# Second layer of a two-layer transformer kernel: maximum scores in row halves of the array, in a burst of two pairs

## The reference

```
q, k, v = LN(x) @ w_Q, LN(x) @ w_K, LN(x) @ w_V          # 16 heads, head size 8
probs   = softmax(q k^T / sqrt(8))                        # over all 512 keys, no mask
x       = x + probs v
xq      = fp4_quant_dequant(LN(x))                        # blocks of 16
h       = silu(xq @ w_gate^T) * (xq @ w_up^T)             # 352 features
x       = x + fp4_quant_dequant(h) @ w_down^T
```

## Time and profile before

| | us |
|---|---|
| three runs | 2309.03, 2312.15, 2314.53 (median 2312.15) |
| profiled execution | 2317.76 (span 2316.0, first to last instruction) |
| PE busy | 2038.6 (88%) |
| DVE busy | 1621.9 (70%) |
| ACT busy | 1390.4 (60%) |
| POOL busy | 1063.4 (46%) |

### The profile page before, as it was taken

How to read it: one execution, slowest core, us unless ns; L and a number is a source line. 1 busy time by engine, 2 the same in 40 slices (tenths; PEclk the granted TensorE clock), 3 DMA queues, 4 the chain that set the end, 5 groups by cost and what they waited for, 6 DMA issues and landing times.

```text
span 2316.0 us, 45088 instructions
## 1 busy us (share of the span) xinstructions
PE 2038.6 (88%) x13603; PEld 1060.0 (46%) x13603; DVE 1621.9 (70%) x4772; ACT 1390.4 (60%) x3097; POOL 1063.4 (46%) x1777
## 2 busy tenths in 40 slices
PE   2999999999999939999649999999999999999984
PEld 1455455554554429999613333333333333333333
DVE  3888888887888633321137888888888888888854
ACT  0466666666666624444207777777777776777772
POOL 6433746537455250000265656555565655654222
PEclk8899999999999969999859999999999999999997
DMA  5232223223222024444322222121222212121100
GB/s 175 81 93 67 85 74 91 73 71 92 71 89 82 20 73 143 144 142 140 90 73 66 73 58 68 54 62 54 66 59 57 70 55 60 55 64 50 47 6 14
DMA packets 154335, 174.12 MB, mean 75 GB/s; under 512 B 38448, under 2 KB 122096, under 8 KB 153968
## 3 DMA queue, kind: packets, MB, share of 16 engines
q1 hardware_dynamic: 144464, 153.85, 22.6%
q0 software_dynamic: 8192, 16.79, 2.5%
q10 hardware_dynamic: 1440, 0.60, 0.1%
HBM read 120.30 MB, written 49.28 MB: 73 GB/s over the span
## 4 chain that ended last, share of the span: by engine, by line
PE 27%; DVE 12%; issue 5%; ACT 4%; POOL 2%; DMA 0%; SPq 0%; ACTq 0%; DVEq 0%; POOLq 0%
PE bank L1560 8%; PE bank L1538 6%; DVE l_rowmax L1770 6%; PE bank L1548 6%; ACT l_probs L1679 3%; DVE l_h L1790 1%; PE bank L1593 1%; PE bank L1574 1%; DVE l_hq L199 1%; PE bank L1631 1%; DVE l_hq L216 1%; DVE l_stats L1804 1%; DVE l_hq L222 1%; PE bank L1621 1%; PE bank L1579 1%
## 5 line engine op out<-in xcount | busy, mean ns | idle before, releaser
L1770 DVE TENSOR_REDUCE l_rowmax<-bank 128x1 f32<-128x512 f32 x1024 | 642.7, 682 | 109.6 <-PE bank L1538 109.4
L1679 ACT ACTIVATE l_probs<-bank 128x512 f32<-128x512 f32 x1024 | 549.1, 605 | 134.8 <-PE bank L1548 134.5
L865 DVE CUSTOM_DVE_ANT_0 bank<-bank,mask_rows_q 128x512 f32<-128x512 f32 (+3 forms) x1024 | 476.6, 518 | 101.9 <-PE bank L625 95.6
L781 ACT ACTIVATE l_probs<-bank 128x512 f32<-128x512 f32 (+3 forms) x1024 | 389.2, 443 | 150.0 <-PE bank L637 144.0
L1538 PE MATMUL bank<-k_stack,q_stack 96*128 96x512 bf16 x1024 | 395.0, 387 | 68.9 <-DVE l_rowmax L1770 43.9
L1548 PE MATMUL bank<-q_stack,k_stack 128*128 128x512 bf16 x1024 | 387.3, 382 | 1.6 <-ACT l_probs L1679 1.4
L625 PE MATMUL bank<-k_stack,q_stack 96*128 96x512 bf16 (+3 forms) x1024 | 316.8, 314 | 25.4 <-DVE l_rowmax L865 14.8
L635 PE MATMUL bank<-q_stack,k_stack 128*128 128x512 bf16 (+3 forms) x1024 | 307.6, 308 | 0.2
L1560 PE MATMUL bank<-l_probs,v_aug 128*32 128x512 f32 x2048 | 272.8, 605 | 29.4 <-ACT l_probs L1679 28.7
L637 PE MATMUL bank<-mask_rows_k,ident_bf 128*128 128x128 bf16 x1024 | 221.1, 221 | 0.0
L1174 ACT ACTIVATE experts_hT<-bank,experts_b 128x256 f32<-128x256 f32 x288 | 118.3, 471 | 158.2 <-PE bank L1136 158.2
(11 more groups left out here) (259 smaller groups left out, 3015.7 us busy)
## 6 DMA issues: line engine op xcount, KB each, us to landing
q_stack<-scratch SPq DMA_DIRECT2D x384, 96.0 KB
k_stack<-scratch SPq DMA_DIRECT2D x384, 96.0 KB
experts_w<-in_w SPq DMA_DIRECT2D x72, 256.0 KB, 2.4
scratch<-l_q_parts SPq DMA_DIRECT2D x32, 384.0 KB, 2.7
scratch<-l_k_parts SPq DMA_DIRECT2D x32, 384.0 KB, 3.0
experts_rows<-rows_in SPq DMA_DIRECT2D x72, 128.0 KB, 2.1
rows_out<-experts_y SPq DMA_DIRECT2D x72, 128.0 KB, 2.1
q_stack<-l_rowmaxT SPq DMA_DIRECT2D x384, 4.0 KB
```

The costliest lines, as they stand in the source:

```text
L781: nc.scalar.activation(probs[:, (a * HG + j) % PSLOTS, c0:S], bank[:, c0:S], ACT.Exp, scale=SCALE).then_inc(t_read, 1)
L865: nc.vector.tensor_tensor_reduce(scores, scores, m["mask_rows_q"][:, S - keys(t):S], 1.0, LOWEST, ALU.add, ALU.max, rowmax[:, g % 2, c:c + ...
L1679: nc.scalar.activation(probs[:, (a * HG + j) % PSLOTS, :], bank[:, :], ACT.Exp, scale=SCALE).then_inc(t_read, 1)
L1770: nc.vector.tensor_reduce(rowmax[:, g % 2, c:c + 1], bank[:, :], X_AXIS, ALU.max).then_inc(s_read, 1)
```

## The change

1. A head's stack is laid out by its place in the group. Heads 0 and 1 stay as they were. Heads 2 and 3 have their first eight blocks on rows 64 to 127, the ninth on rows 0 to 7, and their maximum on rows 32 to 34. The stack of a group takes 14 DMAs (`stack_parts`) of two heads each instead of six of four heads, and the maximum rows take six (`stack_max`) instead of three. The bytes are the same; the rows copied are 2 KB long instead of 4 KB.
2. The maximum scores use 64 rows: heads j and j + 2 are multiplied one behind the other, the first in rows 0 to 63 and the second in rows 64 to 127 of the array, each into its own bank of a pair of banks. The ninth block (the product of the two smallest parts) is left out of the maximum, not out of the exponential. One DVE instruction reads both banks and writes two maxima.
3. Ring "s" is two pairs of banks, ring "t" has three banks.
4. The order on PE in a slot is: exponential products 0 and 1, both pairs, the MIDDLE table, exponential products 2 and 3, `probs_v` of the slot before, the END table. "out" moves from MIDDLE to END, two up products share a pair of banks and one DVE read, AHEAD is 10, and `rowmax`, `split_max` and `max_out` stand one slot later.
5. In experts, DVE sets the constant rows of heads 2 and 3 with six memsets in four consecutive tiles.

Layer zero keeps its code and its banks.

```diff
+def stack_parts(sp, stacks, scratch, g, stacked):
+    for which, stack in enumerate(stacks):
+        for half in range(2):
+            slots = g * HG + 2 * half
+            base = which * PARTS * P * S + slots * S
+            def copy(row, part, step, blocks):
+                sp.dma_start(stack[row:row + blocks * D, slots:slots + 2, :].rearrange("p h t -> p (h t)"),
+                             bass.AP(scratch.tensor, base + part * P * S, [[step * P * S, blocks], [H * S, D], [1, 2 * S]])
+                             ).then_inc(stacked, 16)
+            for i in range(PARTS):
+                blocks = PARTS if half == 0 or i < PARTS - 1 else PARTS - 1
+                if which == 0:
+                    copy(HALF * half + SLAB * i, i, 0, blocks)
+                else:
+                    copy(HALF * half + SLAB * i, 0, 1, blocks)
+            if half:
+                copy(0, PARTS - 1, 0, 1)
+def stack_max(sp, stack, rowmaxT, g, max_rows):
+    for half in range(2):
+        slots = g * HG + 2 * half
+        for i in range(PARTS):
+            row, src = MAX_ROWS[half] + i, (2 * i + half) * 2 * TT
+            sp.dma_start(stack[row:row + 1, slots:slots + 2, :].rearrange("p h (t q) -> p (h t) q", q=P),
+                         rowmaxT[src:src + 2 * TT, :]).then_inc(max_rows, 16)
...
+S_PAIRS = 2
+T_BANKS_1 = 3
-AHEAD = 9
+AHEAD = 10
...
+            def upper_constants(i):
+                stack = (*m["k_stack"], *m["q_stack"])[i]
+                rows_of = lambda first, end: stack[first:end, :, :].rearrange("p (g j) t -> p g (j t)", j=HG)[:, :, 2 * S:4 * S]
+                nc.vector.memset(rows_of(0, HALF).bitcast(U32), 0).then_inc(stack_set, 1)
+                if i < 2:
+                    dve.wait_ge(stack_set, i + 1)
+                    nc.vector.memset(rows_of(MAX_ROWS[1], MAX_ROWS[1] + PARTS).bitcast(F32), MINUS_ONES)
...
-    MIDDLE = [("rowmax", g, 4 * g + 5) for g in range(G)] + [("out", g, F + 4 * g + 8) for g in range(G)] + [
+    MIDDLE = [("rowmax", g, 4 * g + 6) for g in range(G)] + [
         ("xnT", 0, -15), ("xqT", 0, F + 32)] + [("turn", k, F + 44) for k in range(NC)]
-    END = [("v", 0, 0), ("qk", 0, -9), ("qk", 1, -8)]
-    for t in range(TT):
-        END += [("gate", t, F + 33)] + ([("up", t - 1, F + 33)] if t else [])
-    END += [("up", TT - 1, F + 33), ("down", 0, F + 45), ("down", 1, F + 53)]
+    END = [("out", g, F + 4 * g + 6) for g in range(G)] + [("v", 0, 0), ("qk", 0, -9), ("qk", 1, -8)] + [("gate", t, F + 33) for t in range(2)] + [("up", 0, F + 33)] + [
+        ("gate", t, F + 33) for t in range(2, TT)] + [("up", 1, F + 33), ("down", 0, F + 45), ("down", 1, F + 53)]
...
-    POOL_WORK = [("split_max", g, 4 * g + 4) for g in range(G)]
+    POOL_WORK = [("split_max", g, 4 * g + 5) for g in range(G)]
...
-    SP_WORK = [("max_out", g, 4 * g + 6) for g in range(G)] + [("parts", 0, -6), ("parts", 1, -5)]
+    SP_WORK = [("max_out", g, 4 * g + 7) for g in range(G)] + [("parts", 0, -6), ("parts", 1, -5)]
...
+            def scores_for_max(a, pair):
...
+                banks = s_pair(("max", a, pair))
                 t = TT - 1 - t
-                nc.tensor.matmul(bank[:, :], q_stack[b % 2][0:MAXROW, h_, t * P:(t + 1) * P],
-                                 k_stack[b % 2][0:MAXROW, h_, :], start=True, stop=True).then_inc(s_mm, 1)
+                for half in range(2):
+                    rows, h_ = slice(HALF * half, HALF * (half + 1)), g * HG + pair + 2 * half
+                    last = nc.tensor.matmul(banks[:, half * S:(half + 1) * S], q_stack[b % 2][rows, h_, t * P:(t + 1) * P],
+                                            k_stack[b % 2][rows, h_, :], start=True, stop=True)
+                last.then_inc(s_mm, 1)
...
                     if j == HG // 2:
-                        if uses.exp_quad(s - 1) is not None:
-                            probs_v(uses.exp_quad(s - 1))
+                        if a is not None:
+                            for pair in range(2):
+                                scores_for_max(a, pair)
                         for kind, b, k in due(MIDDLE, s):
...
                     if e is not None:
                         scores_for_exp(e, j)
-                    if a is not None:
-                        scores_for_max(a, j)
+                if uses.exp_quad(s - 1) is not None:
+                    probs_v(uses.exp_quad(s - 1))
                 for kind, b, k in due(END, s):
+                    if kind == "out":
+                        turned_out(b, k)
...
+            def take_max(a, pair):
...
+                largest = rowmax[:, g % 2, :].rearrange("p (k i t) -> p i k t", k=2, t=TT)[:, pair, :, TT - 1 - t]
+                nc.vector.tensor_reduce(largest, banks[:, :].rearrange("p (k n) -> p k n", k=2), X_AXIS, ALU.max).then_inc(s_read, 1)
```

More of the change, by code:

```diff
@@ L255, with __init__ @@
 T_BANKS = 4
-AHEAD = 9
+S_PAIRS = 2
+T_BANKS_1 = 3
+AHEAD = 10
 class Uses:
-    def __init__(self, NB, middle, end, ring_of, first, last, ahead, only):
+    def __init__(self, NB, middle, end, ring_of, first, last, ahead, only, pairs):
         self.NB, self.ahead, self.only = NB, ahead, only
@@ L273, in __init__ @@
                 if j == HG // 2:
+                    if self.max_quad(s) is not None and pairs:
+                        for pair in range(2):
+                            use("s", ("max", self.max_quad(s), pair))
                     for key in self.due(middle, s):
@@ L277, in __init__ @@
                     use("t", ("exp", self.exp_quad(s), j))
-                if self.max_quad(s) is not None:
+                if self.max_quad(s) is not None and not pairs:
                     use("s", ("max", self.max_quad(s), j))
@@ L1590, in turned_out @@
                 pe.wait_ge(oT_ready, b * G + g + 1)
-                bank = s_bank(("out", b, g))
+                bank = s_pair(("out", b, g))
                 for t in range(TT):
@@ L1608, in gate, with up @@
                                  start=True, stop=True).then_inc(t_mm, 1)
-            def up(b, t):
-                bank = s_bank(("up", b, t))
-                nc.tensor.matmul(bank[:, 0:HID], xqT[:, t * P:(t + 1) * P], m["w_in_T"][:, 1, :],
-                                 start=True, stop=True).then_inc(s_mm, 1)
+            def up(b, k):
+                pair = s_pair(("up", b, k))
+                for i in range(2):
+                    t = 2 * k + i
+                    last = nc.tensor.matmul(pair[:, i * S:i * S + HID], xqT[:, t * P:(t + 1) * P], m["w_in_T"][:, 1, :],
+                                            start=True, stop=True)
+                last.then_inc(s_mm, 1)
             def turned_hq(b, k):
@@ L1645, in _ @@
                                 turned_max(b, k)
-                            if kind == "out":
-                                turned_out(b, k)
                             if kind == "xqT":
@@ L1793, in read @@
                         dve.wait_ge(h_scaled, b)
-                    last = hw.largest(tile, k, TT)
-                    if k == TT - 1:
+                    last = hw.largest(tiles, k, 2)
+                    if k == 1:
                         last.then_inc(h_step, 1)
@@ L1811, in _ @@
             for s in slots:
-                for j in range(HG):
-                    if j == HG // 2:
-                        for kind, b, k in due(MIDDLE, s):
-                            if RING[kind] == "s":
-                                read(kind, b, k)
-                    if uses.max_quad(s) is not None:
-                        take_max(uses.max_quad(s), j)
+                if uses.max_quad(s) is not None:
+                    for pair in range(2):
+                        take_max(uses.max_quad(s), pair)
                 for kind, b, k in due(END, s):
@@ L1884, in build @@
         m["experts_loaded"] = mem.sem("experts_loaded")
-        psum = [ctx.enter_context(nc.psum_tensor(f"bank{i}", [P, S], F32)) for i in range(8)]
+        m["bank_pairs"] = [ctx.enter_context(nc.psum_tensor(f"pair{i}", [P, 2 * S], F32)) for i in range(2)]
+        psum = [pair[:, k * S:(k + 1) * S] for pair in m["bank_pairs"] for k in range(2)]
+        psum += [ctx.enter_context(nc.psum_tensor(f"bank{i}", [P, S], F32)) for i in range(4, 8)]
         with ExitStack() as until_experts:
```

88 lines of the change are left out of this document (41 added, 47 removed).

## The result

The changed kernel takes 2295.53 us (median of 5 runs, 2289.19 to 2300.3) against 2314.53 for the kernel before (5 runs on the same chip, 2309.03 to 2316.15): ratio 0.9924, 95% interval [0.9901, 0.9948]. It is faster, by 19 us, where 51 were forecast. The profiled executions are 2295.53 and 2317.76, so the traces have 22.2 us to explain.

A forecast was written before the change was run, and what follows sets the result against it. Gates, then DVE, then PE were taken to bound each period. Terms: periods -54, SP queue +2, start and end +1 and -1, constants +1, sum -51: 2267 us profiled, 2261 median; 8-in-10 range 2230 to 2318.

The forecast's parts named there:

- the limits of the three stretches: In one period: first the gate, SiLU, up chain for 6.5 us, then DVE for 21.5, then PE for 38.6.
- the +2 for the queue of SP at the layer's start: Layer's start: more DMA issue time, partly beside the first stack's landing, makes PE wait +2 us (0 to +5).
- the period of 62.9 us: One 16-slot period: gates 6.6, DVE stretch 22.9, PE stretch 33.4, sum 62.9 us, 3.6 less than 66.57.
- A pair saves 0.25 us a slot: PE slot: overlapping halves, two pairs at 0.22 plus mode changes 0.09 and 0.10, give 2.59 us instead of 2.83.
- The 0.28 for a pair: PE: an estimate from a guide's 3.07 times for four row tiles, adding 0.12 a slot, some 15 us in all.
- A read of two banks starts every 1.14 us: DVE maximum reads: 1.14 us from start to start, so 2.28 a slot against 2.4; bounds 1.07 and 1.20.
- Some 15 such periods: Second layer: some 15 periods, each 3.6 us shorter, giving -54 us.
- The rival *queue of SP: Two groups' stacks, then six maximum rows, issued in sequence make PE wait 5.6 us a period: +84, 2345 us; chance 0.14.
- Constants, +1 (0 to +4): Experts: six memsets of 1.8 us over four tiles; two in one tile outlast a gap, +1 us (0 to +4).
- the halves do overlap: Rival claimed the opposite: halves don't overlap, each PE-stretch slot 0.44 us longer, 62 us in all, 2323; chance 0.08.
- the rows have the mode cost: Rival claimed no mode cost for row tiles: pairs save 0.44 a slot, 20 us less, 2241; chance 0.15.
- ACT's waits did not eat half: Rival claimed waits eat half: PE waits 0.2 us a slot more in the PE stretch, 27 us, 2288; chance 0.20.

The follow-up runs named there:

- E12: The changed kernel run once more, beside three variants on one chip: 2294.2 us, ratio 0.9906 to the kernel before.
- E13: Changed kernel's order, ring and two-bank reads, but products on 96 rows, 6 and 3 DMAs a group, no memsets: 2305.69 us, ratio 0.9953.
- E7: Changed kernel with statistics, factors and the normalising product of the next batch one slot later: 2291.76 us, ratio 0.9898.
- E1: Kernel before with 20 DMAs a group (stack in 14 instead of 6, maximum rows in 6 instead of 3): 2410.77 against 2383.57 us, ratio 1.0122.
- E8: Changed kernel with 6 stack and 2 maximum-row DMAs, statistics and normalising one slot later, memsets in six tiles: 2272.46 us, ratio 0.9817.
- E14: Changed kernel with 8 DMAs a group, statistics and normalising one slot later, memsets in six tiles, run on another chip: 2271.54 us, ratio 0.9804.
- E3: Changed kernel with both products of a pair read from rows 0 to 63, so they can't overlap: 2427.11 us, ratio 1.0175.

## Why the prediction was half right

The direction, the saving by the halves and the limits of the three stretches came out as forecast; the size was less than half of it. Two terms of the sum were wrong: the +2 for the queue of SP at the layer's start (step 5) and the period of 62.9 us (step 3). By its own steps:

1. *A pair saves 0.25 us a slot*: right. L1592 to a pair 0.31, pair to pair 0.22, pair to L1592 0.31, entry to L1604 0.31; a plain slot without a wait is 2.61 to 2.64 us from one L1604 block to the next (forecast 2.59; 2.85 before, where 2.83 was taken). The 0.28 for a pair, worked out from four row tiles, did not appear. The halves alone take off 2.09 a period (E12 against E13), where nine slots of 0.25 are 2.25.
2. *A read of two banks starts every 1.14 us*: right (1.08 to 1.14, mostly 1.13; one read 1.216).
3. *The period*, 62.9: it is 64.67. Gates 7.27 for 6.6, DVE stretch 23.45 for 22.9, PE stretch 33.95 for 33.4. The DVE stretch holds the collision of two engines, 0.86 us on the quotient, that the prediction did not see; without it (E7) the period is 63.83, and the other 0.9 us stays unexplained by any one row. The gain was set against 66.57, which should have been 67.41. So two errors met, the new period taken 1.77 too short and the old one 0.84: with 66.57 put right, the same forecast would have been 4.5 us a period. Of the 14 us missing over the twelve periods some 10 come from this, and some 4 from three late periods with falls of the clock.
4. *"Some 15 such periods"*: twelve are whole. Of the last three intervals the first shrank by 2.8 us (63.79 to 60.98), the second by 0.2, and the third grew by 0.9.
5. *"At the layer's start nothing hides it ... I take +2 (0 to +5)"*: this is the step that failed most. I counted the issue time of the first group only, and PE's wait for the first stack, which did not change: from the first write of the parts to the first maximum product 15.76 us before and 15.48 after. What I left out is that the stacks of later groups stand ahead of the maximum rows of earlier ones: three waits, 13.6 us, and a low clock after them. By E1 the step from 9 to 20 DMAs costs some 13 us at the start (the estimate above); going from 20 to 8 takes off 16.5 (E8 against E7). The rival *queue of SP* named the mechanism, stacks of two groups and then six maximum rows, and the price by the DMA was about right (a stack 7.5 us of issue for the forecast 8.4, six rows of maxima 4.05 for 3.7). But I placed it in every period, where it has slack and no wait appears, and not where the prologue runs ahead.
6. *Clock*: not in the prediction. A fall costs 1.5 to 1.6 us; the changed kernel has two among its twelve periods (the three late ones are 4.5 us over 64.67 together) and some at the start.
7. *Constants, +1 (0 to +4)*: the experts took 2.5 to 4 us more in three traces of the changed kernel (355.8 to 357.1 against 353.0 and 353.3). PE waits once 1.5 and once 1.1 us for the copy behind two memsets of 1.76 in one tile. With one memset a tile (E8, E14) the part takes 351.6 to 351.9, but not by the memsets alone: some 2.5 us less stand ahead of the first write of the parts, and 1.9 behind it, where the first stack now comes in six DMAs.

Of the shortfall in the traces, 28.8 us: start 16, twelve periods 14, end 3, experts 2, and layer zero gave 6 back by chance. The other rivals: the halves do overlap; the rows have the mode cost; ACT's waits did not eat half, L1604 no longer waits for the exponential at all.

Left open: why the periods of E1 grew, what else makes a period 64.67 and not 62.9, and what makes the falls of the clock come in two of three periods.

## What to carry to other kernels

Count DMAs by the issue, and look for the place where their queue has no slack: a prologue that runs several stages ahead stacks them in front of what is wanted next, even where the steady state has room; laying the data out in DRAM in the order of the target rows cuts their number. When products get shorter in a stretch that VectorE bounds, nothing is gained there and TensorE's clock may fall; price the stretch behind it at the lower clock. Moving a step on VectorE moves it beside another step of GpSimd: look at what stands there.

## What the runs showed of the hardware

- Products on rows 0 to 63 and 64 to 127 start 3 to 4 ns apart and run fully side by side; going into the 64-row mode and out of it costs 0.09 to 0.10 us each, also when only one half is used (E3).
- Halving a copy hardly cuts SP's time to issue it. From start to start the three copies of 96 KB in the earlier trace rows take 0.78 us each for q and 0.42 for k, but the first of a burst is the longest; copy by copy, the later ones of 24 rows take 0.68 to 0.70 (q) and 0.34 to 0.36 (k) at 96 KB, and 0.68 and 0.36 to 0.37 at 48 KB. Three copies of 72, 64 and 8 rows without a repeated part cost 1.3 to 1.5 together (E14).
- VectorE's product of two SBUF operands, 128x1408, takes 1.59 us alone and 2.45 beside GpSimd's products, of which the one that starts first keeps its 1.04 and the one behind it goes from 1.04 to 2.30. With statistics and product one slot later (E7) the raised pass takes 1.83 instead of 1.61, and GpSimd's product stays at 2.30.
- A memset of 2048 words took 1765 ns on 3 rows and on 64 alike (one of 4096 took 3472):

```profile
L1255 DVE MEMSET k_stack<- 64x2048 uint32 x2 | 3.5, 1765 | 0.7 <-issue 0.7
L1258 DVE MEMSET k_stack<- 3x2048 f32 x2 | 3.5, 1765 | 1.0 <-DVE k_stack L1255 1.0
```
